# Attention steps in pairs, a fifth P buffer and another share of the low parts, in an attention and deformable convolution block

## The reference

```python
x = x + attention(_gn(x), w_qkv, w_proj, b_proj)
x = x + deform_conv_bn_gelu(_gn(x), proj_w, ..., gamma, beta)

# attention: 8 heads of 48 channels over 1024 pixels
attn = jnp.einsum('bhnd,bhmd->bhnm', q, k) * SCALE
attn = jax.nn.softmax(attn, axis=-1)
out = jnp.einsum('bhnm,bhmd->bhnd', attn, v)
out = out @ w_proj.T + b_proj
# second block: offsets and masks from 3x3 convolutions, bilinear samples at 9 shifted
# positions, a product with proj_w, batch normalisation over all images, exact gelu
```

## Time and profile before

| | |
|---|---|
| median of 3 runs | 3647.55 us |
| profiled execution, its own time | 3643.52 us |
| span of the profile (first to last instruction) | 3641.7 us |
| mean granted TensorE clock, of 2.4 GHz | 0.964 |
| TensorE busy | 3294.1 us, 90% |
| VectorE busy | 2295.2 us, 63% |
| ScalarE busy | 1666.2 us, 46% |
| GpSimd busy | 1277.1 us, 35% |

### The profile page before, as it was taken

How to read it: one execution, slowest core, us unless ns; L and a number is a source line. 1 busy time by engine, 2 the same in 40 slices (tenths; PEclk the granted TensorE clock), 3 DMA queues, 4 the chain that set the end, 5 groups by cost and what they waited for, 6 DMA issues and landing times.

```text
span 3641.7 us, 88959 instructions
## 1 busy us (share of the span) xinstructions
PE 3294.1 (90%) x33434; PEld 1908.4 (52%) x33434; DVE 2295.2 (63%) x3770; ACT 1666.2 (46%) x2684; POOL 1277.1 (35%) x1183
## 2 busy tenths in 40 slices
PE   5898999989999899989999899998999989997991
PEld 3254555555555555545556455554555545554660
DVE  5965676756766576755757567675676656765333
ACT  4264444544454443644437344464344544463443
POOL 0161333523343232622327133361334423352440
PEclk9799999999999999999999999999999999998996
DMA  4000001000010000100010000100001000001007
GB/s 135 18 3 36 1 1 38 26 12 1 2 38 37 1 2 2 38 36 1 2 38 3 36 2 1 38 2 36 1 2 38 37 1 2 2 21 70 1 2 312
DMA packets 12151, 97.80 MB, mean 27 GB/s; under 512 B 2777, under 2 KB 2905, under 8 KB 4972
## 3 DMA queue, kind: packets, MB, share of 16 engines
q1 hardware_dynamic: 9468, 67.41, 4.8%
q0 software_dynamic: 1152, 12.58, 0.8%
q10 hardware_dynamic: 1008, 11.01, 0.8%
HBM read 56.26 MB, written 34.60 MB: 25 GB/s over the span
## 4 chain that ended last, share of the span: by engine, by line
PE 53%; issue 21%; POOL 15%; DVE 6%; ACT 3%; DMA 1%; DVEq 0%; POOLq 0%; SPq 0%; ACTq 0%
PE R L1533 20%; POOL PL L619 14%; PE R L1514 12%; PE G L1276 6%; PE G L1309 5%; PE G L1502 2%; PE R L1426 2%; DVE MXP L1016 2%; PE R L1351 1%; DVE M L1205 1%; ACT PL L855 1%; PE G L1494 1%; PE G L1453 1%; PE G L1448 1%; PE R L1412 1%
## 5 line engine op out<-in xcount | busy, mean ns | idle before, releaser
L1533 PE MATMUL R<-P,WALL 128*128 128x512 f16 x3888 | 980.7, 379 | 0.3 <-issue 0.3
L619 POOL TENSOR_TENSOR PL<-P 128x1024 f16<-128x1024 f32 x256 | 573.2, 2243 | 571.8 <-ACT P L778 569.7
L1016 DVE TENSOR_REDUCE MXP<-G 128x1 f32<-128x512 f32 x926 | 629.8, 687 | 163.6 <-PE G L1309 159.3
L1514 PE MATMUL R<-MHL,XB 128*128 128x240 f16 (+14 forms) x7776 | 723.6, 235 | 2.6 <-DVE P L1226 2.5
L656 POOL TENSOR_TENSOR MHL<-M,MHL 128x280 f16<-128x280 f32 (+2 forms) x576 | 364.6, 635 | 855.7 <-ACT MHL L865 854.3
L778 ACT ACTIVATE P<-R 128x1024 f32<-128x1024 f32 x512 | 520.8, 1023 | 242.1 <-PE R L1351 235.0
L1514 PEld LDWEIGHTS R<-MHL,XB 128*128 128x128 f16 x7776 | 571.9, 98 | 105.6 <-DVE P L1226 2.8
L1533 PEld LDWEIGHTS R<-P,WALL 128*128 128x128 f16 x3888 | 378.6, 98 | 395.0 <-issue 0.5
L1066 DVE TENSOR_TENSOR PL<-P 128x1024 f16<-128x1024 f32 x256 | 453.2, 1770 | 180.0 <-ACT P L778 179.8
L1351 PE MATMUL R<-QK 48*128 48x512 f16 (+1 forms) x3072 | 438.9, 395 | 53.3 <-issue 31.6
L1205 DVE TENSOR_TENSOR M<-G,PL 128x240 f32<-128x240 f32 (+17 forms) x864 | 251.3, 319 | 279.7 <-ACT PL L855 162.9
(11 more groups left out here) (142 smaller groups left out, 3530.7 us busy)
## 6 DMA issues: line engine op xcount, KB each, us to landing
XA<-x SPq DMA_DIRECT2D x8, 1536.0 KB, 9.5
X<-x SPq DMA_DIRECT2D x8, 1536.0 KB, 6.5
x_scratch<-X SPq DMA_DIRECT2D x7, 1536.0 KB, 5.1
y_scratch<-XP ACTq DMA_DIRECT2D x7, 1536.0 KB, 7.2
WALL<-y_scratch SPq DMA_DIRECT2D x6, 1536.0 KB, 14.8
out<-WALL POOLq DMA_DIRECT2D x6, 1536.0 KB, 10.8
QK<-x_scratch SPq DMA_DIRECT2D x4, 1536.0 KB, 16.9
P<-wd SPq DMA_DIRECT2D x9, 576.0 KB, 5.0
```

The source lines that it names most:

```text
L619: pool.tensor_tensor(PL[:, s % P_BUFS, :], P32[:, s % P_BUFS, :], high_view(s), ALU.subtract).then_inc(p_low_pool, 1)
L1016: dve.reduce_max(MXP[:, name[1] % 2, n // 2, n % 2:n % 2 + 1], chunk(sec, name)[:, :], AX.X).then_inc(dve_read, 1)
L1514: last = pe.matmul(out, XT[:, x_part, g * BOX_Y + r, t * 128:(t + 1) * 128], MHL[:, m_part, o + at:o + at + (hi - lo) * (x1 - x0)], start= ...
L1533: last = pe.matmul(R6[:, CT + ct, :], WALL[:, w:w + 128], PHL[:, u % 2, part // 2, t, :], start=(u % TAPS == 0 and n < CT), stop=(u % TAPS ...
```

## The change

The stream of TensorE goes over the steps two at a time. It writes `scores(s)` and `scores(s + 1)`, then the chunks of both, then `pv(s - 3)` and `pv(s - 2)`, s being even. In the drain two chunks stand together ahead of `pv(61)` and `pv(62)`, and one ahead of `pv(63)`. P has five buffers in place of four: the fifth fp32 buffer lies in `MHL`, the fifth low buffer in `HL`, which are idle in this stage. GpSimd makes the low part of every third step (2, 5, 8, ...: 21 of 64) and VectorE the other 43. GpSimd's small power follows its first low part after step 18, which is now that of step 20, and VectorE's group shift moves from step 20 to step 22.

```diff
--- before.py
+++ after.py
@@ -29,7 +29,7 @@
 W_SCALE = 256.0
 W_UN = 1.0 / W_SCALE
 MAX_ROW, MAX_UNIT = HD, 16.0
-P_BUFS, LAG = 4, 3
+P_BUFS, LAG = 5, 3
 PAD = HW + 2
 STEPS = HEADS * QT
 UNITS = 2 * TAPS
@@ -106,7 +106,7 @@
     return divmod(u * per_unit(reach) + c + ring(reach), per_unit(reach))
 
 
-GROUPS_AT, SHIFT_AT = 18, 20
+GROUPS_AT, SHIFT_AT = 18, 22
 STATS_AT = {4 + 2 * n: n for n in range(2 * CT)}
 NORM_AT = {24: 0, 32: 1, 40: 2}
 TRANSPOSE_AT = {38: ("oT", 0, 0), 39: ("oT", 0, 1), 54: ("oT", 1, 0), 55: ("oT", 1, 1), 61: ("oT", 2, 0)}
@@ -278,8 +278,8 @@
 
 
 
-DVE_STEPS = [s for s in range(STEPS) if s % 2 == 0]
-POOL_STEPS = [s for s in range(STEPS) if s not in DVE_STEPS]
+POOL_STEPS = [s for s in range(STEPS) if s % 3 == 2]
+DVE_STEPS = [s for s in range(STEPS) if s not in POOL_STEPS]
 
 START_LINKS, BATCH_LINKS = 3, 19
 GN_LINKS = 3
@@ -311,8 +311,8 @@
         QH, QL, KH, KL = [QK4[:, n, :, :] for n in range(4)]
         QZ = sb("QZ", [128, 2, 2, PIX], fp16)
         VS = sb("VS", [128, QT, HEADS, VCOL + 1], fp16)
-        P32 = sb("P32", [128, P_BUFS, PIX], fp32)
-        PL = sb("PL", [128, P_BUFS, PIX], fp16)
+        P32 = sb("P32", [128, CT + 1, PIX], fp32)
+        PL = sb("PL", [128, CT + 1, PIX], fp16)
 
         TAPW = CT * CH
         WALL = sb("WALL", [128, (2 * TAPS + 2) * TAPW], fp16)
@@ -358,6 +358,9 @@
         XF32 = M32[:, 0:PIX]
         CLIP, MSK = M32[0:BOTH, 0:HALF], M32[0:BOTH, HALF:2 * HALF]
         MHL = sb("MHL", [128, 2, M_COLS], fp16)
+        PBUF = [P32[:, n, :] for n in range(CT + 1)]
+        PBUF.append(MHL[:, :, :].rearrange("p a n -> p (a n)")[:, 0:2 * PIX].bitcast(fp32))
+        PLOW = [PL[:, n, :] for n in range(CT + 1)] + [HL[:, :, :].rearrange("p a n -> p (a n)")]
 
         WDH, WDL, WVO = 0, TAPS * TAPW, 2 * TAPS * TAPW
         SELP, SELM, SELY, SELX, ZERO = 0, TAPS, 2 * TAPS, 2 * TAPS + BOX_Y, 2 * TAPS + BOX_Y + BOX_X
@@ -493,7 +496,7 @@
 
         def high_view(s):
 
-            return P32[:, s % P_BUFS, :].bitcast(bf16).rearrange("p (n two) -> p n two", two=2)[:, :, 1]
+            return PBUF[s % P_BUFS].bitcast(bf16).rearrange("p (n two) -> p n two", two=2)[:, :, 1]
 
         def slot(u, c, reach):
 
@@ -616,9 +619,9 @@
 
                 for s in POOL_STEPS:
                     pool.wait_ge(p_exp, b * STEPS + s + 1)
-                    pool.tensor_tensor(PL[:, s % P_BUFS, :], P32[:, s % P_BUFS, :], high_view(s),
+                    pool.tensor_tensor(PLOW[s % P_BUFS], PBUF[s % P_BUFS], high_view(s),
                                        ALU.subtract).then_inc(p_low_pool, 1)
-                    if not final and s == GROUPS_AT + 1:
+                    if not final and s == min(k for k in POOL_STEPS if k > GROUPS_AT):
                         group_rstd(b * 2 + 2)
                 pool.wait_ge(chunk_full, before_taps(b, final).at(("oT", CT - 1, 1), "F"))
                 zeros = SEL[:, ZERO, 0:PAD].unsqueeze(1).to_broadcast([128, 2 * CT, PAD])
@@ -775,7 +778,7 @@
                     act.wait_ge(scores_full, b * STEPS + s + 1)
                     if s >= P_BUFS:
                         act.wait_ge(pv_done, b * STEPS + s - P_BUFS + 1)
-                    act.activation(P32[:, s % P_BUFS, :], ST[s % 2], ACT.Exp, scale=SCALE).then_inc(p_exp, 1)
+                    act.activation(PBUF[s % P_BUFS], ST[s % 2], ACT.Exp, scale=SCALE).then_inc(p_exp, 1)
                     for name in step_chunks(s, not final):
                         read_chunk(name, sec, b)
                     if not final and s in NORM_AT:
@@ -1063,7 +1066,7 @@
                             next_lower(NORM_AT[s - 1], b + 1)
                     if s in DVE_STEPS:
                         dve.wait_ge(p_exp, b * STEPS + s + 1)
-                        dve.tensor_tensor(PL[:, s % P_BUFS, :], P32[:, s % P_BUFS, :], high_view(s),
+                        dve.tensor_tensor(PLOW[s % P_BUFS], PBUF[s % P_BUFS], high_view(s),
                                           ALU.subtract).then_inc(p_low_dve, 1)
                     if s >= LAG and (s - LAG) % QT == QT - 1:
 
@@ -1370,22 +1373,25 @@
                                   start=(kt == 0 and n == 0), stop=False, skip_group_check=True)
                         pe.matmul(out[:, 0:HD], high_view(s)[:, pixels], VS[:, kt, head, 0:HD],
                                   start=False, stop=False, skip_group_check=True)
-                        last = pe.matmul(out, PL[:, s % P_BUFS, pixels], VS[:, kt, head, HD:VCOL],
+                        last = pe.matmul(out, PLOW[s % P_BUFS][:, pixels], VS[:, kt, head, HD:VCOL],
                                          start=False, stop=(kt == QT - 1), skip_group_check=True)
                     last.then_inc(pv_done, 1)
 
-                for s in range(STEPS + LAG):
+                for s in range(0, STEPS + LAG, 2):
                     if s < STEPS:
                         scores(s)
-                        for name in step_chunks(s, not final):
+                        scores(s + 1)
+                        for name in step_chunks(s, not final) + step_chunks(s + 1, not final):
                             if name[0] == "gn":
                                 group_mean(name, sec, b * 2 + 2)
                             else:
                                 fill_chunk(name, sec, b)
                     elif not final:
-                        fill_chunk(DRAIN[s - STEPS], sec, b + 1)
-                    if s >= LAG:
-                        pv(s - LAG)
+                        for name in DRAIN[s - STEPS:min(s - STEPS + 2, LAG)]:
+                            fill_chunk(name, sec, b + 1)
+                    for k in (s - LAG, s - LAG + 1):
+                        if 0 <= k < STEPS:
+                            pv(k)
                 if not final:
                     fill_chunk(DRAIN[LAG], sec, b + 1)
                 fill_chunk(("oT", CT - 1, 1), sec, b)
```

## The result

The changed kernel is slower: a median of 3663.38 us over five runs (3656.64 to 3669.92) against 3647.55 before, whose range 3641.84 to 3650.81 is of five runs too. The ratio is 1.0047, with a 95% interval of 1.0028 to 1.0065. I had forecast 3636, with a range of 3614 to 3656: the sign is wrong, and the time lies 27 us off, outside the range. The profiled execution took 3667.83 us, its span is 3666.0, and its mean granted clock is 0.952, where before had 0.964.

A forecast was written before the change was run, and what follows sets the result against it. TensorE, busy 90% of the span, was taken as the bound. A middle batch: -5.8 + 1.6 + 2.3 + 0.6 + 0.4 = -0.9 us; the last -5.2; 11.5 less in all, giving 3636 us, range 3614 to 3656.

The forecast's parts named there:

- The pairs' saving: Attention stage: a pair of steps takes 2.75 us instead of 2.93, saving 5.8 us a batch, 46 us in all.
- ScalarE's blocks: Next-image operations after steps 24, 32, 40: TensorE waits 0.6, 1.7, 1.7 us instead of 0.8 each, +1.6 a middle batch.
- the sum: Walked order of four engines: 0.9 us less in each of seven batches, 5.2 less in the last, 11.5 in all.
- The waits: TensorE's waits in a middle batch: ScalarE +1.6 us, low parts +2.3, the transpose of step 61 +0.6.
- The rival's price: Clock rival, chance 0.04: 14 waits of 1.7 us each bring 6.8 us at half clock, 48 us in all, 3684 us.
- if the clock row falls inside a stage: One of the signs named beforehand that would show the forecast wrong: a lowered TensorE clock within an attention stage.
- The moved group shift: VectorE, two steps later: ahead of a point where it has been ready; no cost entered.
- The slower rival by late low parts: GpSimd's even-step low parts come late; gain gone from 3.6 us of waits a batch, six give 3677 us; chance 0.10.
- The total without the two waits for low parts: Products of steps 22 and 46 not waiting: a middle batch gains 3.2 us and the total is 3619 us.

The follow-up runs named there:

- e3: Changed kernel with ScalarE's two operations for the next image behind steps 25, 33, 41 instead of 24, 32, 40: 3629.96 us, ratio 0.9948 to before.
- e4: Changed kernel with zero-matrix matmuls added on TensorE at the four places where it stood idle: 3646.07 us, ratio 0.9993 to before.
- e6: Changed kernel with the changes of e3 and e5 together: 3623.45 us, ratio 0.9938 to before.
- e1: Changed kernel with low parts alternating between VectorE and GpSimd and the group shift at step 20, as before: 3658.40 us, ratio 1.0031 to before.
- e5: Changed kernel with the group shift at step 23, written with one SBUF tensor and a per-partition scalar: 3651.74 us, ratio 1.0012 to before.
- e9: Kernel before with one more 128x1024 ScalarE operation at steps 24, 32 and 40, steps still single: 3708.03 us, ratio 1.0169 to before.

## Why the prediction was wrong

**The pairs' saving held.** Twelve scores in 1.47 us, a pair 2.72 to 2.75, changes of kind halved. The last stage, which has neither ScalarE's blocks nor the group shift, shows it clean: steps 10 to 62 take 73.7 us where they took 78.6. The stage as a whole is 2.8 us shorter against the 5.2 of the sum, since its start has a longer lowered stretch (6.8 us, before none).

**The waits held too.** ScalarE's blocks give waits of 1.53 us at steps 35 and 43, and 0.61 at 27 where the clock had held until there, near the 1.7 and 0.6 worked out; the product of step 22 waits 1.6 for a low part (forecast 1.2), that of step 46 1.0 in three of the six middle stages (forecast 1.1). The idle time of a middle stage is the forecast's 6.3 us within 0.3. Only the first stage idles 2.4 us more than that. The price of those waits as idle time was right; what followed them was not in it.

**The failed step is the clock.** The sum put the clock inside a stage at nothing. The text gave it a chance of 0.04 and dismissed it with one row: after a wait of 1.57 us the clock stayed at 2.4 GHz. The row was read rightly, but one wait without a fall was taken as the rule. In the runs 61 of 111 waits of 1.5 to 2.0 us in the stages were followed by half clock, in one stage and not in the next of the same instructions (e3). Filled waits (e4) or shorter ones (e6) left none. Why one such wait is followed by it and the next is not stays open. The Trainium skill (TensorE: Matmul & The Clock Gate, section on a second failure mode) tells of a kernel whose frequent short idles let the clock go to and fro. The trace agrees that short idle times can bring it; it does not show that they must be frequent, since in e3 a single wait of 1.60 us was enough. The text had also named "if the clock row falls inside a stage" as a sign of being wrong, and that is what the trace showed.

The rival's price was too high, though its kind was right: 14 waits and 3.4 us of loss each give 48 us. Measured, each 3.4 us of stretch costs 1.5 us (e3), and 51.2 us of them cost about 51.2 / 3.4 x 1.5 = 23 us. TensorE's busy time says 20: between steps 10 and 62 it is 77.1 to 78.8 us in the six middle stages, and 74.6 in the first, where the clock held.

**The moved group shift was put at nothing, and was not nothing.** The text said that it stands "ahead of a point where it has been ready". Ready it was, but it reads two SBUF tensors, like a low part, and GpSimd's low part of step 23 held the port: 1.84 us instead of 0.16. It held up VectorE's low part and ScalarE's first block. The move is not what did it, for e1 has 1.60 us at the old step. The Trainium skill (SBUF — State Buffer, section on SBUF's two separate sides) names the kind of operands and no size; the trace agrees, and I had applied it to long operations only. GpSimd's own power took 1.53 us, not 0.55. Curing the shift gains 11.6 us (e5). But the sum of the waits had come out as forecast with the shift in it, and e3 and e6 idle the same 4.5 us. So little of its cost was waiting; it made a wait of 1.6 us, and the half clock behind that was the cost.

**The sum of the miss.** In the profiled executions the stages are 22.4 us longer where 11.5 less were forecast: 34 us. Of these about 20 are the later stretches and 2.4 the first stage's extra waits. The other 11 lie in the stages' first ten steps, which take 6.9 us longer where the sum had 4.4 less (five pairs' 0.18 us in eight stages, less 0.4 in seven); half clock lasts 25 us longer there. The starts are not shown to belong to the change: e3 runs the same instructions up to step 24, and its starts have 67 us at half clock, not 85, and take 8.5 us less. By the medians the miss is 27 us. The profile before was 4 us under its median and the profile after 4 us over, which is chance of two single runs. The gains of the cures nearly add up: the shift 11.6 us, ScalarE's blocks 33.4, both together 39.9.

**Smaller points.** The slower rival by late low parts did not happen as described: in the fourth stage TensorE's waits for VectorE's low parts sum to 2.6 us, less than the 3.6 that it needed. The crowding of the port was there, but in one place. The total without the two waits for low parts is 3620 by the sum's own terms, not 3619.

## What to carry to other kernels

Grouping matmuls of one kind saved 0.18 us for each pair of changes, but work that the single-step order spread out now meets a pair, and waits beside it grow. Price a long wait of TensorE (here 1.5 us and more) as the wait and the half-speed stretch that may follow it (here 1.5 us per 3.4), and do not take one wait without a fall as proof that none will follow. Put side work of another engine behind the last step of a group. A one-column operation with two SBUF tensors queued behind a whole GpSimd operation: look at operand kinds, not at lengths.

## What the runs showed of the hardware

- Of 111 TensorE waits of 1.5 to 2.0 us in the stages of the twelve profiles, 61 were followed by 1.2 GHz for 3.4 or 6.8 us, in some images and not in others of one program (e3, e9). Of 344 shorter ones none was, and with every wait at 1.02 us or below there was no such stretch (e6).
- Adding 35 useless matmuls a stage made the kernel 17 us faster (e4).
- A 128x1 product with two SBUF inputs took 1.84 us beside GpSimd's operation (0.16 before, without one), and 0.20 us beside it with one input and a scalar column (e5).
